# Attention value sum: one float32 product replaced by three float32r passes, with V's low part in the residual's place and the reciprocals spread by GpSimd transfers

## What is computed

```python
q = (x @ wq + bq).reshape(N, H, Dh) * Dh ** (-0.5)
k = (x @ wk + bk).reshape(N, H, Dh)
v = (x @ wv + bv).reshape(N, H, Dh)
scores = jnp.einsum('ehd,ehd->eh', q[src], k[dst])
ex = jnp.exp(scores - smax[src])
attn = ex / denom[src]
out = jax.ops.segment_sum(attn[:, :, None] * v[dst], src, num_segments=N)
return out.reshape(N, D) @ wo + bo
```

## Time and profile before

| | us |
|---|---|
| median of 3 runs | 1890.31 (1885.86 to 1890.96) |
| profiled execution, its own time | 1887.15 |
| span of the profiled execution | 1885.4 |
| TensorE busy | 1826.2, 97% |
| VectorE busy | 1097.7, 58% |
| ScalarE busy | 754.7, 40% |
| GpSimd busy | 327.5, 17% |

### The profile page before, as it was taken

One profiled execution on the slowest core, in us unless ns is written; L12 is line 12 of the kernel. 1 busy time (PEld: TensorE's weight loads), 2 busy tenths in 40 slices (PEclk: granted clock), 3 DMA queues, 4 the chain that ended last, 5 costly groups with the idle time before them and its releaser, 6 DMA issues.

```text
span 1885.4 us, 31958 instructions
## 1 busy us (share of the span) xinstructions
PE 1826.2 (97%) x11066; PEld 1521.3 (81%) x11067; DVE 1097.7 (58%) x2302; ACT 754.7 (40%) x1071; POOL 327.5 (17%) x393
## 2 busy tenths in 40 slices
PE   6899999999999999989999999899999999999998
PEld 6887554687888888878888888788888887888887
DVE  6888546634555667345555773355547834555476
ACT  4553221024565431235654412255543212556532
POOL 0000721300000434000003440000016400000163
PEclk9999999999999999999999999999999999999999
DMA  3002200121000110211001011101010112000011
GB/s 120 0 0 98 95 28 34 44 78 56 29 29 1 39 51 23 78 44 38 33 1 39 23 51 54 67 15 44 14 39 23 51 37 83 15 29 29 23 66 66
DMA packets 38731, 79.64 MB, mean 42 GB/s; under 512 B 10856, under 2 KB 10856, under 8 KB 38592
## 3 DMA queue, kind: packets, MB, share of 16 engines
q1 hardware_dynamic: 38592, 77.82, 12.4%
HBM read 66.14 MB, written 11.67 MB: 41 GB/s over the span
## 4 chain that ended last, share of the span: by engine, by line
PE 63%; issue 32%; DVE 1%; ACT 1%; DVEq 1%; POOL 1%; DMA 1%; ACTq 0%; SPq 0%; POOLq 0%
PE ps L1278 39%; PE ps L1303 5%; PE ps L1210 4%; PE ps L1336 4%; PE ps L1268 4%; PE ps L1329 2%; PE ps L1237 2%; PE ps L1342 2%; PE ps L1387 2%; DMA x<-in_x_dram 1%; DVE hot L850 0%; POOL film L527 0%; DVEq L845 0%; PE ps L1391 0%; POOL kh L573 0%
## 5 line engine op out<-in xcount | busy, mean ns | idle before, releaser
L1303 PE MATMUL ps<-pT,v 128*128 128x256 f32 (+1 forms) x1600 | 370.2, 379 | 4.1 <-ACT pT L764 4.1
L703 ACT ACTIVATE s<-masked_s,small 128x1280 f32 (+1 forms) x156 | 213.3, 1367 | 338.2 <-DVE small L983 338.2
L1278 PE MATMUL ps<-yT,w 128*128 128x512 f32 (+1 forms) x1728 | 330.1, 352 | 0.0
L1303 PEld LDWEIGHTS ps<-pT,v 128*128 128x128 f32 x1600 | 292.2, 190 | 42.3 <-ACT pT L764 8.4
L1278 PE MATMUL ps<-kh,q_parts 128*128 128x512 f32 (+3 forms) x1440 | 317.4, 365 | 4.8 <-DVE v L1065 3.4
L1278 PEld LDWEIGHTS ps<-yT,w 128*128 128x128 f32 x1728 | 280.6, 189 | 45.0
L1278 PEld LDWEIGHTS ps<-kh,q_parts 128*128 128x128 f32 (+1 forms) x1440 | 248.5, 189 | 51.7 <-issue 4.8
L1278 PE MATMUL ps<-w,kh 128*128 128x512 f32 (+1 forms) x960 | 235.4, 396 | 2.4 <-POOL kh L573 2.4
L764 ACT COPY pT<-ps 128x1408 f32<-128x1408 f32 (+1 forms) x160 | 206.7, 1292 | 3.9 <-PE ps L1391 3.9
L1278 PEld LDWEIGHTS ps<-w,kh 128*128 128x128 f32 (+1 forms) x960 | 174.3, 186 | 41.3 <-POOL kh L573 2.8
L980 DVE CUSTOM_DVE_ANT_0 masked_s<-ps,mask 128x1280 f32<-128x1280 f32 x96 | 143.2, 1491 | 91.3 <-PE ps L1278 91.3
(11 more groups left out here) (167 smaller groups left out, 1983.9 us busy)
## 6 DMA issues: line engine op xcount, KB each, us to landing
mask<-mask_dram SPq DMA_DIRECT2D x24, 640.0 KB, 4.0
w_raw<-in_L_gnn_m_w_dram SPq DMA_DIRECT2D x8, 1024.0 KB, 5.3
mask_y<-mask_dram SPq DMA_DIRECT2D x12, 640.0 KB, 4.6
mask_dram<-mask_out SPq DMA_DIRECT2D x10, 640.0 KB, 2.9
w_l<-in_L_gnn_W_dram SPq DMA_DIRECT2D x2, 2048.0 KB, 10.1
w_raw<-in_L_gnn_wq_dram SPq DMA_DIRECT2D x4, 1024.0 KB, 5.4
w_raw<-in_L_gnn_wk_dram SPq DMA_DIRECT2D x4, 1024.0 KB, 5.4
w_raw<-in_L_gnn_wv_dram SPq DMA_DIRECT2D x4, 1024.0 KB, 6.2
```

The lines of the kernel that those rows point to most:

```text
L703: nc.scalar.activation(to, masked_of(u), ACT.Exp, bias=small[0:R, u % 2, 1:2], accum_out=small[0:R, u % 2, 2:3]).then_inc(exp_done, 1)
L1278: mine = mm(to, left(a), right(b), start=first and n == 0, stop=final and n == 2)
L1303: mine = mm(ps[:, 6 + gh % 2, 0:wd], v[:, t, h * P:(h + 1) * P], pT[:, gh % 2, t, 0:wd], start=(t == 0), stop=(t == NT - 1))
```

## The change

The value sum becomes three float32r passes (low V by high weights, high by high, high V by low weights; fifteen matmuls of 256 columns in a unit). V is now kept as a high part `v` and a low part `v_low`. VectorE writes the sum `v_sum`, ScalarE copies the high part, VectorE subtracts in place. `v_sum` and `v_low` lie in the place of x from tile 2.5 on, so x is written to DRAM before each attention (`spill_x`, on SP) and read back: tiles 0 and 1 after unit 0, tiles 2 to 9 after the last head output. `s_first` lies in the first 2.5 tiles of x.

The turned weights get a high and a low part: ScalarE copies each unit in two halves of five tiles, now ahead of the exponential of u+1, and VectorE subtracts each half from PSUM (`weights_low`). The halves stand in banks 3 and 4, and 5 and 6; both pairs' value sums share bank 7, so a value sum waits for the head output of the pair before. The turning of `rep` on TensorE and the three small operations on VectorE go. GpSimd makes the reciprocals (a maximum and a power of -1 on 128 values), writes them to DRAM by a transfer of its own, waits for it, and reads them back over all partitions by another; it also takes over the low part of the queries. `masked_s` gets two places, shared with the exponentials, and the masks get four places in place of five.

The core of the diff (float32r types, sizes and semaphores left out; `turn_bank`, `sums` and `turned_places` only give the places named above; GpSimd's `q_part` is VectorE's, moved):

```diff
-MASK_PLACE = (0, 1, 2, 3, 4, 0, 2, 3, 4, 0)
+MASK_PLACE = (0, 1, 2, 3, 0, 2, 3, 0, 2, 3)
+HALVES = (range(0, NT // 2), range(NT // 2, NT))
...
-        v = at("v", 0, "v", [P, NT, D])
+        v = at("v", 0, "v", [P, NT, D], F32R)
+        v_low = at("x", 5120, "v_low", [P, NT, D], F32R)
+        v_sum = at("x", 5120, "v_sum", [P, NT, D])
         yT = at("yp", 0, "yT", [P, 2, KD, NP], F32R)
-        pT = at("yp", 0, "pT", [P, 2, NT + 1, 2 * P])
+        pT = at("yp", 0, "pT", [P, 2, NT + NT // 2, 2 * P], F32R)
         masks = [at("y", 0, "mask_y", [P, NP]), at("w", 0, "mask_w", [P, NP])] + [
-            at("yp", 22528 + 5120 * n, f"mask_{n}", [P, NP]) for n in range(3)]
+            at("yp", 30720 + 5120 * n, f"mask_{n}", [P, NP]) for n in range(2)]
...
-        masked_s = at("w", 26656, "masked_s", [P, NP])
-        s_first = at("s_first", 0, "s_first", [P, NP])
+        masked_s = at("w", 16384, "masked_s", [P, 2, NP])
+        s_first = at("x", 0, "s_first", [P, NP])
+        rep = at("row_bias", 0, "rep", [P, 2, 2 * P])
...
+            def spill_x(i):
+
+                for t in range(NT):
+                    sp.wait_ge(biased, i * 2 * NT + t + 1)
+                    sp.dma_start(x_spill[t * P:t * P + rows(t)], x[0:rows(t), t, :]).then_inc(x_spilled, 16)
+
+            def reload_x(t):
+                sp.dma_start(x[0:rows(t), t, :], x_spill[t * P:t * P + rows(t)]).then_inc(x_back[t], 16)
...
+                    if t == 4:
+                        sp.wait_ge(turned, i * U + 1)
+                        reload_x(0)
+                        reload_x(1)
+                    if t >= 4:
...
                 sp.wait_ge(turned, i * U + U)
                 load_w("M1", m_w1, i)
+                sp.wait_ge(head_out, i * GH + GH)
+                for t in range(2, NT):
+                    reload_x(t)
...
+            def reciprocals(gh, i):
+
+                g = gh // H
+                for k in range(2):
+                    R = rows(2 * g + k)
+                    pool.wait_ge(exp_done, i * U + 2 * gh + k + 1)
+                    pool.sem_inc(passed)
+                    nc.gpsimd.tensor_scalar(small[0:R, k, 3:4], small[0:R, k, 2:3], 0.5, None, ALU.max).then_inc(den_s, 1)
+                    pool.wait_ge(den_s, i * U + 2 * gh + k + 1)
+                    nc.gpsimd.tensor_tensor(rec[0:R, gh % 2, k:k + 1], small[0:R, k, 3:4], minus_one[0:R, :],
+                                            ALU.pow).then_inc(rec_ready, 1)
+                    pool.wait_ge(rec_ready, i * U + 2 * gh + k + 1)
+                    pool.sem_inc(passed)
+                    nc.gpsimd.dma_start(rec_dram[gh % 2, k * P:k * P + R].rearrange("(p o) -> p o", o=1),
+                                        rec[0:R, gh % 2, k:k + 1]).then_inc(rec_saved, 16)
+
+            def spread_reciprocals(gh, i):
+
+                g = gh // H
+                wd = rows(2 * g) + rows(2 * g + 1)
+                pool.wait_ge(rec_saved, (i * GH + gh + 1) * 32)
+                pool.sem_inc(passed)
+                if gh >= 2:
+                    pool.wait_ge(head_out, i * GH + gh - 1)
+                pool.sem_inc(passed)
+                nc.gpsimd.dma_start(rep[:, gh % 2, 0:wd], rec_dram[gh % 2:gh % 2 + 1, 0:wd].broadcast_to([P, wd])).then_inc(rep_in, 16)
+
+            def pool_attention(i):
+
+                for gh in range(GH):
+                    reciprocals(gh, i)
+                    if gh + 2 < GH:
+                        q_part(gh + 2, i)
+                    spread_reciprocals(gh, i)
...
                 split_film(2 * i + 1)
+                pool_attention(i)
...
-                if u >= 3:
-                    act.wait_ge(turned, i * U + u - 1)
+                if u >= 2:
+                    act.wait_ge(rec_ready, i * U + u - 1)
...
+                    if kind == "V":
+                        act.wait_ge(dve_out, c.dve + jl.dve_out[kind, a, b])
+                        nc.scalar.copy(v[0:rows(a), a, :], v_sum[0:rows(a), a, :]).then_inc(v_high, 1)
...
+                    R = rows(2 * g + k)
+                    act.wait_ge(turned, i * U + u + 1)
+                    for half in range(2):
+                        nc.scalar.copy(pT[:, 0, turned_places(gh, half), k * P:k * P + R], turn_bank(half, R)).then_inc(p_high, 1)
                     if u + 1 < U:
                         exp(u + 1, i)
                     if u == U - 1:
                         act.wait_ge(scored, i * U + U)
                         split_head_outputs(0, i)
                         split_head_outputs(1, i)
-                    R = rows(2 * g + k)
-                    act.wait_ge(turned, i * U + u + 1)
-                    if gh >= 2 and k == 0:
-                        act.wait_ge(head_out, i * GH + gh - 1)
-                    turn = ps_flat[:, 3 * BANK:3 * BANK + (NT + 1) * P].rearrange("p (t r) -> p t r", r=P)
-                    nc.scalar.copy(pT[:, gh % 2, :, k * P:k * P + R], turn[:, :, 0:R]).then_inc(pT_out, 1)
...
+            def v_low_part(t, i):
+
+                dve.wait_ge(v_high, i * NT + t + 1)
+                R = rows(t)
+                nc.vector.tensor_tensor(v_low[0:R, t, :], v_sum[0:R, t, :], v[0:R, t, :].bitcast(F32),
+                                        ALU.subtract).then_inc(v_ready, 1)
+
+            def weights_low(u, i):
+
+                gh, k = u // 2, u % 2
+                R = rows(2 * (gh // H) + k)
+                for half in range(2):
+                    places = turned_places(gh, half)
+                    dve.wait_ge(p_high, (i * U + u) * 2 + half + 1)
+                    nc.vector.tensor_tensor(pT[:, 1, places, k * P:k * P + R], turn_bank(half, R),
+                                            pT[:, 0, places, k * P:k * P + R].bitcast(F32), ALU.subtract).then_inc(p_ready, 1)
...
-                if u >= 1:
-                    dve.wait_ge(exp_done, i * U + u)
+                if u >= 2:
+                    dve.wait_ge(turned, i * U + u - 1)
...
-                dve.wait_ge(pT_out, i * U + 2 * gh + 2)
-                nc.vector.tensor_tensor(q[:, h, g * 2 * P:g * 2 * P + wd], ps[:, 6 + gh % 2, 0:wd],
-                                        pT[:, gh % 2, NT, 0:wd], ALU.mult).then_inc(head_out, 1)
+                dve.wait_ge(rep_in, (i * GH + gh + 1) * 16)
+                nc.vector.tensor_tensor(q[:, h, g * 2 * P:g * 2 * P + wd], sums(gh, wd),
+                                        rep[:, gh % 2, 0:wd], ALU.mult).then_inc(head_out, 1)
...
+                            dve.wait_ge(x_spilled, (c.block + 2) * NT * 16)
+                        nc.vector.tensor_tensor(v_sum[0:R, a, :], bank[0:R, :], row_bias[0:R, 0, :],
                                                 ALU.add).then_inc(dve_out, 1)
+                        if a >= 1:
+                            v_low_part(a - 1, c.block + 1)
...
+                        if not second:
+                            dve.wait_ge(x_back[a], c.block * 16 + 16)
...
-                    dve.wait_ge(exp_done, i * U + u + 1)
-                    nc.vector.tensor_scalar(small[0:R, u % 2, 2:3], small[0:R, u % 2, 2:3], 0.5, None,
-                                            ALU.max).then_inc(den_s, 1)
-                    dve.wait_ge(den_s, (i * U + u) * 2 + 1)
-                    nc.vector.reciprocal(small[0:R, u % 2, 3:4], small[0:R, u % 2, 2:3]).then_inc(den_s, 1)
-                    dve.wait_ge(den_s, (i * U + u) * 2 + 2)
-                    if u >= 1:
-                        dve.wait_ge(turned, i * U + u)
-                    nc.vector.tensor_scalar(rep[0:R, :], ident[0:R, :], 0.0, small[0:R, u % 2, 3:4], ALU.mult,
-                                            ALU.add).then_inc(rep_ready, 1)
                     if u + 1 < U:
                         mask(u + 1, i)
-                    if k == 1 and u // 2 + 2 < GH:
-                        q_part(u // 2 + 2, i)
+                    if u == 0:
+                        v_low_part(NT - 1, i)
                     if k == 1 and u >= 2:
                         head_output(u // 2 - 1, i)
+                    weights_low(u, i)
...
+                weights = (i * U + 2 * gh + 1) * 2 + part + 1
+                pe.wait_ge(p_high, weights)
                 if part == 0:
-                    pe.wait_ge(pT_out, i * U + 2 * gh + 2)
-                    if gh >= 2:
-                        pe.wait_ge(head_out, i * GH + gh - 1)
-                for t in range(5 * part, 5 * part + 5):
-                    mine = mm(ps[:, 6 + gh % 2, 0:wd], v[:, t, h * P:(h + 1) * P], pT[:, gh % 2, t, 0:wd],
-                              start=(t == 0), stop=(t == NT - 1))
+                    if gh == 0:
+                        pe.wait_ge(v_ready, i * NT + NT)
+                    if gh >= 1:
+                        pe.wait_ge(head_out, i * GH + gh)
+                place = turned_places(gh, part).start - HALVES[part][0]
+                for n, (a, b) in enumerate(((1, 0), (0, 0), (0, 1))):
+                    if b == 1:
```

(51 more changed lines are left out.)

47 lines of the change are left out of this document (26 added, 21 removed).

## The result

The changed kernel takes 2130.92 us (2114.98 to 2132.5, four runs) against 1890.47 for the kernel before, measured in turn: 1.126 times as long, 95% interval 1.122 to 1.130. The forecast was 1838, with a range of 1812 to 1885. It was wrong in size and in sign.

What follows compares the result with a forecast made beforehand. TensorE's chain was taken to bound the kernel. Per block, attention gains 20.9 us, its end loses 5.3 and the clock 2.5, leaving 13.1; four blocks give 52.4, so 1890.3 becomes 1838 us, range 1812 to 1885.

Steps and rivals of the forecast that it cites:

- w: Landing of the reciprocals' store that GpSimd waits for in attention: taken as 2.9 us, farthest row 5.3.
- GpSimd's loop: GpSimd's work for one pair of units, 1.8 + 3d + w: 7.7 us, against two units of 8.70.
- d: GpSimd's time to issue one transfer in attention: chosen as 1.0 us, between 0 and 1.29.
- The lock-out: VectorE blocking GpSimd's descriptor writes in attention: if it held, about 1.5 us per issue, loop 12, well past 1944 us.
- Rival A: GpSimd sets the pace in attention and the kernel is slower: 1944 us, loss from a loop of 9.5 on; 12%.
- A unit: One unit of attention on TensorE: 1.74 + 1.80 + 0.81 = 4.35 us, against 4.948 before.
- rival D: Value sum: fifteen passes cost 0.144 us each or more, taking as long as the float32 sum; 1890 us, 3%.
- rival B: VectorE's chain in a unit is longer than 4.34 us, its margin being 0.10; 1860 us, 17%.
- The start of a block: First value sum of an attention: its wait for a queued copy goes; 1.5 us gained.
- The end of attention: WO starts 6.2 us after the last transpose's start instead of 0.9: loss 5.3 us, between 3.3 and 8.3.
- The clock: TensorE's granted clock falls after the gap before WO: 2.5 us lost per block, bounds 0 and 3.4.
- Rival C: The clock holds through the gap before WO: 10 us less, 1828 us; 8%.

Runs made afterwards that it cites:

- e10: The same three transfers and early split as e8_row_tail, but issued by GpSimd instead of SyncE; 1920.96 us, 1.017 of the kernel before.
- e8_row_tail: e6 with ScalarE also splitting head outputs 0 and 1 ahead of the last unit's copies; 1816.44 us, 0.962 of the kernel before.
- e1: Changed kernel without the reciprocals' store and the wait for it, the spread reading an input row; 1834.41 us, 0.970 of the kernel before.
- e6: Changed kernel with SyncE moving reciprocals: pieces into an SBUF row, row to DRAM as one piece, then spread; 1828.44 us, 0.968 of the kernel before.
- e3: Changed kernel with the 4-byte pieces stored 512 bytes apart in DRAM, the spread reading an input row; 1844.57 us, one run.

## Why the prediction was wrong

**The step that failed is w**, the landing of the store in GpSimd's loop, taken as 2.9 with a bound of 5.3. It was 6.9 in the median and 7.9 in the pair shown. The 2.9 was that of 640 KB in long rows, and 5.3 that of a load. Neither shared what the new store has: 128 writes of 4 bytes next to each other. I took the distance between two unlike rows for the uncertainty; it was no bound, because the property that mattered was in neither row. The fixed 2.0 us of the Trainium skill (DMA: Bandwidth & Descriptors, Anatomy of one DMA), which I had quoted beside it, is about what the same store took once its pieces were 16 bytes apart (1.8) or in SBUF (2.0); the change as written took more than three times that.

**The other terms of the loop held.** Two reciprocals with their issues are 4.3 us and the spread's issue 0.6 (e10's rows), so 1.8 + 3d is 4.9 and d 1.0, as chosen; of it 0.62 is the issue and the rest the gap ahead of it. With w of 6.9 (the median) to 8.6 (from issue to spread in the pair shown) the loop is 11.8 to 13.5; the units of the kernel after are 6.1 to 6.3 apart, 12.4 for a pair.

The issues themselves show no sign of being held up; the store's in the kernel after, by tile (duration ns min/median/max):

```profile
L630 POOL DMA_DIRECT2D rec_dram<-rec x160: 617/620/786, 443.2 to 2014.2; - x160
```

160 issues beside VectorE's reads of PSUM, 0.79 us at most. The lock-out of which the Trainium skill speaks (DMA: Bandwidth & Descriptors, SWDGE vs HWDGE vs iDMA), which by the prediction's estimate would have made each about 1.5 us longer, doesn't show here. No row says which mode VectorE was in, so the rule itself isn't tested.

**Rival A was the right mechanism with too small a price.** Its own formula, fed with 12.4: 18 pairs x (12.4 - 9.9) = 45, the end 5.3 + 4.0, the clock 3.4, less 1.5 for the start: 56 per block, 2115 us. Measured: 45.3, 14.2, 2.2, less 0.9 for start and other stages, 61 in all. Its turning point was put at 9.5, so that a loop of 9.6 would cost some 7 us; e10, with 9.6, is 30 us slower (1.7%). Its units gain 4.1 us a block, but with three landings behind one another the gap ahead of WO 0 loses 10.2 and the clock 2.0. I gave the rival 12% on the word of the 2.9 alone.

**A unit.** Forecast 4.35, measured 4.417. The chain of e8_row_tail, two units:

```profile
527.98 0.42 PE ps L1502 x5
528.41 1.78 PE ps L1385 x9
530.19 1.79 PE ps L1418 x15
531.98 0.81 PE ps L1502 x10
532.79 1.82 PE ps L1385 x9
534.61 1.78 PE ps L1418 x15
536.39 0.82 PE ps L1502 x10
537.21 2.01 PE ps L1385 x9
```

Fifteen passes 1.78 to 1.79 (forecast 1.80: rival D falls), ten transposes 0.81 (0.81), nine score matmuls 1.78 to 1.82 where I took 1.74 from rows 2. What adds the 0.06, I can't say. In some units it is 2.01: there VectorE's mask ends at 537.11, after a split of wo that stood before it, and the scores wait for it. So rival B's margin of 0.10 is real and just holds; its excess shows only in such units. Units 3 to 39 gain 17.5 us a block, forecast 19.4.

**The start of a block.** Forecast a gain of 1.5. In blocks 0 and 3 the distance from the last record of unit 0 to that of unit 2 is 9.1 us against 11.0 and 10.9: 1.8 gained. In blocks 1 and 2 it seems to have grown, in e8_row_tail to 11.5 and 14.8 from 10.6. Block 1, timeline of that kernel, and under it VectorE in the kernel before:

```profile
805.11 1.29 ACT L865 CAST pT<-ps 128x640 fp32r<-128x640 f32 x2 [3.85 <-issue]
...
805.24 1.49 DVE L1093 CUSTOM_DVE_ANT_0 masked_s<-ps,mask_w 128x1280 f32<-128x1280 f32 x1 [4.04 <-issue]
...
806.79 2.01 PE L1385 MATMUL ps<-kh,q_parts 128*128 128x512 f32 x9 [2.95 <-DVE small L1093]
```
```profile
822.56 0.15 DVE L1118 TENSOR_SCALAR small<-small 128x1 f32<-128x1 f32 x1 [4.34 <-issue]
```

At the head of the loop ScalarE and VectorE stand for some 4 us with nothing that the profile shows. That pause is in the kernel before as well (4.34 us), only ahead of unit 0's turned reciprocals instead of behind its transposes, so the distance is no fair measure there. Starts and other stages together gain 4.9 us of span in e8_row_tail, against 6 forecast; but the same account gives 1.3 for e1, 6.5 for e6 and 10.6 for e3, so the runs scatter too much to confirm it. What the engines wait for in the pause, no run tests. The DMA view of e8_row_tail from 800 to 805.3 us counts three packets of the instruction queues, against twelve in the 100 us from 450 to 550, so a fetch of instructions is a candidate, not shown.

**The end of attention.** Forecast WO at +6.2 from the last transpose's start with a landing of 2.9, against +0.9 before. In e3_apart, where nothing collides but the last store, issued 0.34 us behind a load of 1 MB on SyncE, lands in 5.4 instead of 1.8, it is +8.6; in the kernel after +13.1 to +18.0. Two paths lie under it, as forecast: GpSimd's, and ScalarE's at +3.2 (e1, forecast +3.5). e6 takes the first away (16 us against e3), e8 the second (12 us more).

**The clock.** Forecast: it falls in the gap and costs 2.5 a block. In the kernel after WO 0 takes 4.54 to 5.49 instead of 3.02, 2.2 a block; with gaps of 2.9 (e6) 2.1. Rival C falls. The clock can fall behind a gap of 1.08 us too: in e8 WO 0 takes 3.02, 4.62, 3.02 and, behind 1.24 us, 4.35. e8's windows after the first and the second attention, columns as in rows 9:

```profile
611.90:615.00 3.10, 2.74 (x12) 2.28 (x13) 1.17 (x2) 2.44 (x5) 2.60 (x3) 1.00 0.02 0
...
978.10:983.00 4.90, 4.65 (x14) 3.68 (x15) 1.05 (x2) 2.33 (x5) 2.50 (x3) 0.65 0.23 33
```

The same gap, a granted clock of 1.00 once and 0.65 the other time.

**That e1 came to 1834 where 1838 was forecast is partly luck.** Its units gain 69.9 of span, starts and other stages 1.3, gaps and clock lose 9.5 and 8.0: 53.7, where the forecast had 52.4, but as 83.6 gained and 31.2 lost, and in e1 the landing that made most of that loss was left out. The forecast is better held against e3, 1844.57, 7 us above it. e8's own account: units 69.8 and starts with the rest 4.9 gained, gaps 2.1 and clock 3.0 lost, 69.6 of span.

## What to carry to other kernels

A new transfer is priced by a row that shares its shape, above all the size of its pieces and how they lie in memory; where there is none, the loop that waits for it deserves a wide range, and the first run a look at the landing. 4-byte pieces from 128 partitions shouldn't be stored side by side in DRAM: gather them in a row of SBUF (2.0 us) and store that as one piece, or leave 16 bytes. A chain of waits on landings goes to a queue whose engine has nothing else to do: with the same three transfers the kernel takes 1816 us on SyncE's queue and 1921 on GpSimd's.

## What the runs showed of the hardware that was not expected

- 128 writes of 4 bytes to DRAM land 1.8 us after issue when they are 16, 64 or 512 bytes apart, 3.5 at 8 bytes, 7.3 side by side, 2.0 into a row of SBUF; while the slow one of the pair shown was outstanding the DMA engines were idle. Issued by SyncE, side by side is slow as well (units of 5.7 to 5.9 us, against 4.42 with the same pieces in a row of SBUF).
- GpSimd takes 0.62 us to issue 128 pieces of 4 bytes, 0.52 for one piece, 0.57 for a spread over 128 partitions, and about 0.58 passes between the end of its own operation and the transfer that waits for it.
- A store of 98 pieces issued 0.33 to 0.54 us behind a load of 1 MB landed in 5.2 to 5.4 us in all four blocks of e3, where the median is 1.8. That the load is the cause is argued, not tested.
- Gaps of 1.08 us on TensorE were followed by a granted clock of 1.00 in one block and 0.65 in another.
